# Retention: the order of VectorE's three rotary multiplications around its addition to X

## The reference

```python
x = x + _L1_attn_ref(_layernorm(x), ...)
...
q = _rotary(x @ Wq.T)          # 8 heads of 64
k = _rotary(x @ Wk.T)
v = x @ Wv.T                   # 8 heads of 128
g = x @ Wg.T
# _rotary: x * cos + concat(-x2, x1) * sin, x1 and x2 the halves of a head
scores = q k^T * 64 ** -0.5 * decay       # per head, causal
o = scores v
o = (o - mean(o)) * rsqrt(var(o) + 1e-5) * gn_weight + gn_bias   # per head
return (o * silu(g)) @ Wo.T
```

## Time and profile before

| what | value |
|---|---|
| median of 3 runs | 1225.07 us (1220.78 to 1226.32) |
| the profiled execution | 1221.82 us |
| its span, first to last instruction | 1220.0 us |
| mean granted TensorE clock | 0.96 of 2.4 GHz |
| retention loop, first to 29th product of L1107 | 525.87 to 810.84 us from the span's start |

### The profile page before, as it was taken

One profiled execution on the slowest core, in us unless ns is written; L12 is line 12 of the kernel. 1 busy time (PEld: TensorE's weight loads), 2 busy tenths in 40 slices (PEclk: granted clock), 3 DMA queues, 4 the chain that ended last, 5 costly groups with the idle time before them and its releaser, 6 DMA issues. The chain is left out here.

```text
span 1220.0 us, 31356 instructions
## 1 busy us (share of the span) xinstructions
PE 1109.4 (91%) x11494; PEld 935.5 (77%) x11494; DVE 812.2 (67%) x1786; ACT 646.8 (53%) x1175; POOL 586.6 (48%) x600
## 2 busy tenths in 40 slices
PE   6989998999999999699999999996899878999970
PEld 4776666779999977578888888886577678899970
DVE  6767997853322443488888888883688766566762
ACT  5516775843566543366666666652687621466640
POOL 5762322115666575473333333343344325676775
PEclk9989999999999999899999999997999979899995
DMA  7014220201233321100000000000111060133342
GB/s 202 10 41 162 60 69 4 74 10 55 71 81 78 102 72 38 33 11 1 0 0 0 0 0 0 0 1 1 19 22 20 5 232 17 56 88 83 86 128 63
DMA packets 59536, 60.78 MB, mean 50 GB/s; under 512 B 12240, under 2 KB 48720, under 8 KB 58928
## 3 DMA queue, kind: packets, MB, share of 16 engines
q1 hardware_dynamic: 49904, 41.63, 11.4%
q0 software_dynamic: 8640, 17.71, 5.9%
q10 hardware_dynamic: 896, 0.17, 0.1%
HBM read 41.77 MB, written 15.60 MB: 47 GB/s over the span
## 5 line engine op out<-in xcount | busy, mean ns | idle before, releaser
L1666 POOL DMA_INDIRECT f_xn<-f_xn_rows,f_source x142 | 138.0, 972 | 41.9 <-issue 40.7
L2057 PE MATMUL f_bank<-f_xT,f_w_tile 128*128 128x128 f32 x1136 | 152.1, 277 | 0.0
L2068 PE MATMUL f_bank<-f_w_down,f_hidden 128*128 x1136 | 150.4, 276 | 0.0
L2057 PEld LDWEIGHTS f_bank<-f_xT,f_w_tile 128*128 128x128 f32 x1136 | 140.6, 195 | 0.0
L2068 PEld LDWEIGHTS f_bank<-f_w_down,f_hidden 128*128 128x128 f32 x1136 | 138.9, 193 | 0.0
L1075 POOL TENSOR_TENSOR ret_rstd<-ret_var,ret_minus_half 128x8 f32<-128x8 f32 x32 | 52.7, 1647 | 157.2 <-DVE ret_var L1115 156.8
L1677 POOL DMA_INDIRECT f_hot_row<-f_slots_y,f_slots x112 | 108.3, 967 | 33.5 <-issue 33.1
L905 PEld LDWEIGHTS a_mixed_psum<-a_v_diag,a_probT 128*64 128x64 f32 x2048 | 65.8, 138 | 59.2 <-ACT a_probT L857 44.5
L767 POOL TENSOR_TENSOR X<-X,a_mixed 128x128 f32<-128x128 f32 x64 | 29.2, 456 | 157.2 <-DVE a_mixed L800 150.8
L1951 ACT ACTIVATE f_w_tile<-f_w_up 128x512 f32 x142 | 87.6, 620 | 28.5 <-DVE f_owner L1850 26.8
L808 DVE TENSOR_REDUCE a_top<-a_scores 128x16 f32<-128x1024 f32 x64 | 78.3, 1224 | 34.0 <-PE a_scores L890 33.0
(11 more groups left out here) (304 smaller groups left out, 2787.0 us busy)
## 6 DMA issues: line engine op xcount, KB each, us to landing
f_slots_y<-f_y_out SPq DMA_DIRECT2D x70, 128.0 KB, 2.2
a_v_rows<-in_ctx SPq DMA_DIRECT2D x16, 256.0 KB, 3.9
f_xn_rows<-f_xn SPq DMA_DIRECT2D x16, 256.0 KB, 6.7
f_w_up<-in_f_up SPq DMA_DIRECT2D x1, 2560.0 KB, 9.0
f_w_down<-in_f_down SPq DMA_DIRECT2D x1, 2560.0 KB, 15.5
f_xn<-f_xn_rows,f_source POOLq DMA_INDIRECT x142, 2.6
X<-in_x SPq DMA_DIRECT2D x4, 512.0 KB, 6.5
kv_ctxT<-in_ctxT SPq DMA_DIRECT2D x8, 256.0 KB, 5.4
```

The source lines that it names most:

```text
L1666: pool.indirect_dma_start(out=x_in[:, s % RING, :], out_offset=None, in_=xn_rows[:, :], in_offset=bass.IndirectOffsetOnAxis(ap=source[:, s ...
L2057: last = pe.matmul(bank_h[m % 3][:, j * P:(j + 1) * P], w_tile[m % W_RING][:, j * P:(j + 1) * P], xT[m % 3][:], start=True, stop=True)
L2068: last = pe.matmul(bank_y[m % 2][:, 0:D].unsqueeze(1), hidden[m % 3][:, j, :], w_down[:, bass.ds(expert + E0, 1), j, :], start=(j == 0), s ...
```

## The change

Within VectorE's step the cosine product and the first sine product change places around the addition to X: the order was cosine, addition, sine, sine, and becomes sine, addition, sine, cosine. `turned_ready` is raised by the cosine, which is the last of them. The waits stay where they were, ahead of the first multiplication and ahead of the addition.

```diff
-                        dve.tensor_tensor(fold(qk[b][:]), src,
-                                          cos[:].unsqueeze(1).to_broadcast([P, 2 * H, R_KEY]), ALU.mult)
+
+                        def turn(part):
+                            to, of = slice(32 * part, 32 * part + 32), slice(32 - 32 * part, 64 - 32 * part)
+                            dve.tensor_tensor(fold(turned[b][:])[:, :, to], src[:, :, of],
+                                              sin[:, to].unsqueeze(1).to_broadcast([P, 2 * H, 32]), ALU.mult)
+                        turn(0)
                     m = s - 4
                     if live(m, N):
                         dve.wait_ge(S["out_in_psum"], m + 1)
...
                     m = s - 1
                     if live(m, N):
-                        for part in range(2):
-                            to, of = slice(32 * part, 32 * part + 32), slice(32 - 32 * part, 64 - 32 * part)
-                            last = dve.tensor_tensor(fold(turned[b][:])[:, :, to], src[:, :, of],
-                                                     sin[:, to].unsqueeze(1).to_broadcast([P, 2 * H, 32]), ALU.mult)
-                        last.then_inc(S["turned_ready"], 1)
+                        turn(1)
+                        dve.tensor_tensor(fold(qk[b][:]), src,
+                                          cos[:].unsqueeze(1).to_broadcast([P, 2 * H, R_KEY]), ALU.mult)\
+                            .then_inc(S["turned_ready"], 1)
```

## The result

The changed kernel takes 1233.66 us (median of 7 runs, 1229.58 to 1235.71) against 1225.07 (7 runs): a ratio of 1.0065, 95% interval 1.0047 to 1.0083, or 8.0 us (5.8 to 10.2). The ratio is taken over all the runs; the two medians alone lie 8.6 us apart. The forecast was 6.8 us more, 1231.9 us.

A forecast was written before the change was run, and what follows sets the result against it. A ring of waits through VectorE, TensorE and ScalarE was taken to bound the kernel. 28 longer steps add 6.39 us, minus 0.12 for the first addition, plus 0.51 at the end: 6.8 on 1225.07, 1231.9 us, range 1226 to 1237.

The forecast's parts named there:

- The older ring: Loop through VectorE, TensorE and ScalarE's gate and affines, said to bind before; after the change 10.29 us, 10.47 with a branch back.
- (a): Addition to X on VectorE: starts 3.49 us after the product, not 3.61, after 0.42 us of idle VectorE.
- (b): VectorE from the addition's start to the end of "decayed": 3.75 us instead of 3.21, as the cosine replaces a sine half.
- (c): TensorE's waits: xn transpose 0.16 us late, L1338 transposes 0.40 late; GpSimd's addition of rotated halves costed at nothing.
- (d): Late L1338 transposes: 0.14 of 0.40 us taken up, 0.26 passed to the output matmuls, giving steps of 10.39 us.
- the new ring: Loop through VectorE and TensorE alone: 3.75 + 0.11 + 4.32 + 2.21 = 10.39 us a step.
- single disturbed step: Loop step before the change where the addition found VectorE idle; source of the 4.32 and 2.21 us TensorE legs.
- The sum: 28 steps, 22 at 10.39 and 6 at 10.47: 6.4 us more; with first and last steps 6.8 us.
- The older ring alone: Rival: ScalarE's affines stay last, late transposes cost nothing; 4.6 us more, 1229.7 us; chance 0.17.
- The stall in full: Rival: VectorE's idle 0.42 us before the addition is lost whole in 28 steps, 11.8 us, 1236.9; chance 0.08.
- The earlier addition: Rival: releasing V's second half 0.12 us earlier gains 3.5 us, 1221.6, up to 10 us; chance 0.09.
- The clock: Rival: new TensorE waits lower its clock; one step in ten at 1.2 GHz adds 14 us, 1246; chance 0.03.

## Why the prediction was right

**What bounds it.** The older ring through ScalarE bound the kernel before: taking 0.38 us out of ScalarE's part brought it to 0.9940, and moving the addition 0.60 later made each step 0.60 longer. The prediction calls the half of V that waits for the addition the second; it is the first half, which stands second in the list.

**(a), the earlier addition.** Put at 3.49 us after the product, measured 3.50 in the step shown, 3.59 and 3.80 in the second and third step and 3.47 to 3.51 in the others; the idle 0.42 us before it is listed as 0.34, since the records of VectorE overlap by 0.08.

**(b), the work behind it.** 3.75 us, measured 3.75.

**(c), who waits.** The xn transpose and L1338 both wait, 0.12 us after their signals where 0.11 was read. GpSimd's addition was costed at nothing and no wait for it appears at TensorE's transposes of q and k: in the step shown it ends at 671.82 and they start at 674.53.

**(d), the new ring.** 10.39 worked out, 10.39 measured, and shown to be the ring that binds by the experiment that shortened ScalarE's and left the steps at 10.39. It rested on a single disturbed step; the steady state repeated its legs.

**The sum.** 6.4 us for the 28 steps were worked out and 7.2 measured. The missing 0.8 lies in three places. Steps with a branch back took 10.55 and not 10.47, six times 0.08: the leg from the xn transpose to the next product is 4.75 us (669.47 to 674.22) where I took 4.67 from a step in which this transpose had not waited. By that the older ring is 10.37, only 0.02 under the new one. The first step took 10.48. And the step with the late start of "normed", 10.59 in the kernel before, takes 10.72, while I had given it 10.39. Against these stands the last step, 0.10 shorter. Behind the loop the transposes of L1338 follow the last addition by 3.87 us and not 3.35, 0.52 where 0.51 was worked out:

```profile
823.58 0.29 DVE L1135 TENSOR_TENSOR X<-ret_ps,X 128x128 f32<-128x128 f32 x1 [0.53 <-PE ret_ps L1290]
```

```profile
827.45 0.86 PEld L1341 LDWEIGHTS ret_ps<-ident,ret_normed 128*128 128x128 f32 x8 [0.47 <-issue]
```

So 7.2 - 0.1 + 0.5 = 7.6 us by the trace in place of 6.8, inside the 5.8 to 10.2 of the runs.

Behind that the two traces can't be compared. After waits of 2.12 us in both, the output matmuls of the 31st tile ran at a granted clock of 0.53 in the kernel before (3.31 us of weights) and at 1.00 in the changed one:

```profile
840.43 1.86 PEld L1290 LDWEIGHTS ret_ps<-ret_wo,ret_gated 128*128 128x128 f32 x16 [2.12 <-DVE ret_gated L1107]
```

From the 29th addition to the last are therefore 29.35 us before and 28.99 after, although the step that the change lengthens takes 9.96 in place of 9.52. Why the clock fell in one and not in the other is not shown.

**The rivals.** The older ring alone fell with the run that shortened it. The stall in full (0.42 us a step) did not come: 0.26 did. The earlier addition earned 0.12 us a step at its own place and lost it at the next wait. The clock stayed at 1.00 over the 28 steps with three waits a step, and also in the two kernels with the longest waits: 0.94 us for the addition with the cosine and a sine ahead, and 0.94 us at the xn transpose with the addition first. The rule of the Trainium skill on micro-idles (TensorE: Matmul & The Clock Gate, section "A second HAM failure mode: psum-queue depth-cycling") was not borne out by these waits.

## What to carry to other kernels

In a loop pipelined over several engines, write down each ring of waits and sum its legs; a step takes the largest. The addition to X was best placed here where its signal had just arrived: earlier, it held back all that is listed behind it on its engine; later, it held back who waits for it. Before taking a gain from releasing something earlier, ask which signals move later in exchange, and how much slack each has.

## What was not expected of the hardware

- After a wait at the xn transpose, the time from its weights to the next product was 4.75 us, in the changed kernel and with the addition first (685.41 to 690.16); without one it was 4.67. The difference lies right behind the transpose: the first gate weights follow its own by 0.13 us after a wait (669.47 to 669.60), and stand at the same time in the record without one (674.23). Why is not shown.
- The opposite holds at L1338: 4.32 us to the output weights after a wait, 4.36 without one.
- The loop's timing repeated to 0.01 us from step to step and from kernel to kernel (10.39 in four of them), while whole executions spread over 6.1 us for the changed kernel and 8.2 us for the one before. Effects of 0.1% could be read from the loop and not from the runs.
